# Four-head pass order, an early gate split before the Runge-Kutta loop, and 41 unread matmuls

## The reference

```python
x1 = ln(x) * (1 + scale1) + shift1                 # ada = cond @ ada_w + ada_b
x  = x + gate1 * (attention(x1, 16 heads of 128) @ out_w + out_b)
x2 = ln(x) * (1 + scale2) + shift2
x  = x + gate2 * (gelu(x2 @ ffn_w1 + b1) @ ffn_w2 + b2)     # block 1

z, h = sigmoid(x @ Wz.T + bz), g(x @ Wn.T + bn)    # block 2, minGRU:
s[t] = (1 - z[t]) * s[t-1] + z[t] * h[t]           # a scan over 32 tokens
drive = input + s

for t in range(32):                                # block 3: 32 RK4 steps
    for stage in range(4):                         # FitzHugh-Nagumo, state q, p
        dq = q - q**3/3 - p + drive[t] + tanh(q) @ coupling.T + bias
        dp = 0.08 * (q + 0.7 - 0.8 * p)
    q, p = clip(...)
    trace[t] = q
out = drive + blocksparse_ffn(trace)               # block 4, top 4 of 16 blocks
```

## Time and profile before

| what | value |
|---|---|
| median of 3 runs | 519.38 us (519.37 to 520.13) |
| the profiled execution: its time, its span | 521.38 us, 519.5 us |
| PE, DVE, ACT, POOL busy | 449.8, 434.4, 314.2, 48.4 us |
| chain that ended last, by engine | DVE 43%, PE 37%, ACT 10%, issue 5%, POOL 2%, DMA 2% |
| attention passes | to about 248 us |
| first and last write of q in the loop | 331.1 us, 507.4 us |

### The profile page before, as it was taken

How to read it: one execution, slowest core, us unless ns; L and a number is a source line. 1 busy time by engine, 2 the same in 40 slices (tenths; PEclk the granted TensorE clock), 3 DMA queues, 4 the chain that set the end, 5 groups by cost and what they waited for, 6 DMA issues and landing times.

```text
span 519.5 us, 13419 instructions
## 1 busy us (share of the span) xinstructions
PE 449.8 (87%) x4832; PEld 310.7 (60%) x4832; DVE 434.4 (84%) x1698; ACT 314.2 (60%) x872; POOL 48.4 (9%) x77
## 2 busy tenths in 40 slices
PE   2999989999999899997498996589797887888886
PEld 2655675557546665566244442478676776767676
DVE  4969876777776876979978776999999999999994
ACT  1378855786487748775467935464655646555563
POOL 2001320224021211042000000000000000000000
PEclk9899999999999999999789999596979879788899
DMA  8972402200202000000000000000000000000000
GB/s 292 415 305 62 105 4 78 61 21 0 81 21 61 0 1 0 0 1 0 0 1 1 0 1 0 3 2 0 2 1 11 11 0 11 1 11 11 1 10 22
DMA packets 10127, 20.82 MB, mean 40 GB/s; under 512 B 1456, under 2 KB 4720, under 8 KB 9456
## 3 DMA queue, kind: packets, MB, share of 16 engines
q1 hardware_dynamic: 9536, 19.89, 11.4%
q10 hardware_dynamic: 560, 0.60, 0.3%
HBM read 19.40 MB, written 1.08 MB: 39 GB/s over the span
## 4 chain that ended last, share of the span: by engine, by line
DVE 43%; PE 37%; ACT 10%; issue 5%; POOL 2%; DMA 2%; ACTq 0%; DVEq 0%
PE bank L765 33%; DVE base L1567 5%; DVE lin L1659 5%; DVE qs L1573 4%; DVE cub L1561 3%; DVE sq L1555 3%; ACT ptx L567 3%; PE score L765 3%; ACT ao_sb L535 2%; DVE pacc L1669 2%; POOL ptx L471 2%; ACT sraw L560 2%; PE spare L765 2%; DMA vec<-vecs 2%; DVE thlo L1551 1%
## 5 line engine op out<-in xcount | busy, mean ns | idle before, releaser
L765 PE MATMUL bank<-x,pairs_store 128*128 128x512 f16 x384 | 87.2, 384 | 0.0
L765 PE MATMUL score<-th,coup_part 128*128 128x32 f16 x1024 | 48.1, 182 | 19.4 <-ACT th L728 17.3
L765 PEld LDWEIGHTS bank<-x,pairs_store 128*128 128x128 f16 x384 | 37.7, 99 | 43.8 <-issue 2.2
L471 POOL TENSOR_TENSOR ptx<-pt,ptx 32x256 f16<-32x256 f32 x64 | 44.5, 696 | 190.8 <-ACT ptx L567 187.2
L535 ACT ACTIVATE big<-bank,pass_b 128x512 f16<-128x512 f32 x64 | 42.1, 683 | 23.5 <-DVE pass_b L1286 15.8
L728 ACT ACTIVATE th<-qs 128x64 f16<-128x64 f32 x96 | 24.4, 254 | 50.5 <-DVE qs L1573 50.5
L765 PEld LDWEIGHTS score<-th,coup_part 128*128 128x128 f16 x1024 | 36.4, 100 | 30.8 <-ACT th L728 29.3
L1298 DVE SCALAR_TENSOR_TENSOR big<-bank,pass_b,big 128x512 f16<-128x512 f32 x64 | 45.2, 739 | 7.5 <-ACT big L535 7.3
L765 PE MATMUL bank<-pairs_store,ao_sb 128*128 128x256 f16 x384 | 46.1, 273 | 5.2 <-DVE ao_sb L1298 1.9
L765 PEld LDWEIGHTS bank<-pairs_store,ao_sb 128*128 128x128 f16 x384 | 35.8, 98 | 12.7 <-DVE ao_sb L1298 4.3
L765 PE MATMUL bank<-pairs_store,x 128*128 128x512 f16 x192 | 43.4, 379 | 0.0
(11 more groups left out here) (197 smaller groups left out, 1017.9 us busy)
## 6 DMA issues: line engine op xcount, KB each, us to landing
wqk_sb<-wqk SPq DMA_DIRECT2D x16, 256.0 KB, 2.9
wv_sb<-wv SPq DMA_DIRECT2D x4, 512.0 KB, 5.7
wo_sb<-wo SPq DMA_DIRECT2D x4, 512.0 KB, 3.9
f_sb<-ffn_w SPq DMA_DIRECT2D x2, 1024.0 KB, 14.1
ao_sb<-xtok SPq DMA_DIRECT2D x4, 256.0 KB, 5.7
big<-ada_w SPq DMA_DIRECT2D x1, 1024.0 KB, 9.6
x_sb<-xT SPq DMA_DIRECT2D x1, 1024.0 KB, 13.4
w_sb<-w1T SPq DMA_DIRECT2D x1, 1024.0 KB, 16.2
```

The lines of the kernel that those rows point to most:

```text
L471: nc.gpsimd.tensor_tensor(ptx[s, 1, :, s], pt[s], ptx[s, 0, :, s], ALU.subtract).then_inc(ptx_ready, 1)
L765: return nc.tensor.matmul(dst, lhsT, rhs, start=start, stop=stop, **kw)
```

## The change

It has three parts.

1. **End of each attention pass.** ACT empties three of the four `project(3)` banks before `exps(2)`, and copies the two strips of scores 3 before `place_high(2)`. DVE does `low_projs(3)` and the first half of `low_pv(1)` before `normalise(2)`, the second half after `shift(3)`; `add_heads(0, 0)` comes after `normalise(3)`, and `add_heads(0, 3)` after `add_heads(1, 0)`.
2. **Gates of the second half and the entry of the loop.** `last_gates` splits piece n = 2 in two halves of 256 tokens, issues the products of feature block k = 0 before the last x3 is there, and puts the first half of Wn's product in `spare`. `min_gru` runs in halves for n = 2; for n = 3 ACT makes `za`. `drive_bias(1)`/`drive_lows(1)` go ahead of `residual(1)`. Of pieces 2 and 3 only the first four time steps are split before the loop; the other 28 go in eight parts into slots of the first iteration that before held a split of h with no use. The two tanh of the first stage stand before the loop, and each later pair at the end of the stage before, so that the loop's back-edge on ACT lies behind them.
3. **Unread matmuls.** 6, 15 and 20 matmuls of 512 fp16 columns whose results nothing reads: after `turn_x2(0)`, after `turn_normed(0)`, and after the last gate.

```diff
-                empty_projs(3, [0])
+                empty_projs(3, (0, 1, 2))
                 exps(2)
-                empty_projs(3, (1, 2, 3))
+                empty_projs(3, [3])
                 empty_pv(1)
+                copy_scores(3, NB4 // 2)
                 place_high(2)
-                copy_scores(3, NB4 // 2)
                 exps(3)
...
+            drive_bias(0, 1)
+            drive_bias(1, 2)
+
+            use = USE_GRU[1]
+            act.wait_ge(half_full, 1)
+            relu_pair(2, 2, first_half, 0, spare, half_ready)
+            wait_product(use + 1)
+            gate_tanh(2, first_half, 0, half_ready)
+            wait_product(use)
+            relu_pair(2, 3, second_half, 0, bank[bank_of(use)], free[bank_of(use)])
+            gate_tanh(2, second_half, 0, free[bank_of(use + 1)])
...
+            nc.scalar.activation(za_last, tz_of[1], ACT.Identity, bias=one_half[:], scale=-0.5).then_inc(za_ready, 1)
+            drive_bias(2, 4)
+            act.wait_ge(q_ready, 1)
+            nc.scalar.activation(th16[:], qn[:].rearrange("p k b -> p (k b)"), ACT.Tanh).then_inc(th16_ready, 1)
+            nc.scalar.activation(th32[:], qn[:].rearrange("p k b -> p (k b)"), ACT.Tanh).then_inc(th32_ready, 1)
+            drive_bias(3, 5, slice(0, UNROLL))
+            drive_bias(3, 5, slice(UNROLL, T))
...
+            def unread(dst, count):
+
+                for _ in range(count):
+                    mm(dst, scaled_eye[:], ptx[:, 0, 0:G // 2].rearrange("p g n -> p (g n)"), True, True)
+
+            pe.wait_ge(eye_ready, 1)
             turn_x2(0)
+            unread(spare[:], 6)
             turn_normed(0)
+            unread(spare[:], 15)
...
+            def last_gates():
+
+                dst = [fill(USE_GRU[1] + w) for w in range(2)]
+                middle = HALF // 2
+                wn_half = (spare[:, 0:middle], dst[0][:, middle:HALF])
+                pe.wait_ge(x3_ready, KB + 1)
+                for c in range(2):
+                    gate(0, c)
+                mm(dst[1][:], wz_sb[:, 0, 0:P], x3[:, 0, HALF:N], True, False)
+                pe.wait_ge(x3_ready, 2 * KB)
+                gate(1, 0).then_inc(half_full, 1)
+                mm(dst[1][:], wz_sb[:, 1, 0:P], x3[:, 1, HALF:N], False, True).then_inc(full[bank_of(USE_GRU[1] + 1)], 1)
+                gate(1, 1).then_inc(full[bank_of(USE_GRU[1])], 1)
...
             output_layer(1)
-            gates(1)
+            last_gates()
+            unread(score[:, 1], 20)
...
                 shift(2)
+                low_projs(3)
+                low_pv(1, [0])
                 normalise(2)
-                low_projs(3)
-                low_pv(1)
                 last_strips()
                 shift(3)
+                low_pv(1, [1])
+                normalise(3)
                 add_heads(0, 0)
-                normalise(3)
                 low_pv(2, [0])
...
+            min_gru(2, 2, first_half, (half_ready, 1), (half_ready, 2))
+            dve.wait_ge(z_used, 3)
+            min_gru(2, 3, second_half, emptied(use), emptied(use + 1))
+            dve.wait_ge(z_used, 4)
+            min_gru(3, 4, every, emptied(use + 2), emptied(use + 3), (za_ready, 1))
+            drive_lows(2, 3, slice(0, UNROLL))
+            drive_lows(3, 4, slice(0, UNROLL))
```

More of the change, by code:

```diff
@@ L133, in build @@
         eps_gelu = sb("eps_gelu", [P, 1])
+        one_half = sb("one_half", [P, 1])
         x1 = sb("x1", [P, KB, N])
@@ new lines, in gate_tanh, with wait_product @@
+            def gate_tanh(n, cols, ob, ready):
+                nc.scalar.activation(tz_of[n % 2][:, cols], bank[bank_of(USE_GRU[n // KB] + 2 * ob + 1)][:, cols], ACT.Tanh,
+                                     bias=hb[:, ob:ob + 1], scale=0.5).then_inc(ready, 1)
+            def wait_product(use):
+                act.wait_ge(full[bank_of(use)], count_of(use))
+            every, first_half, second_half = slice(0, HALF), slice(0, HALF // 2), slice(HALF // 2, HALF)
+            for ob in range(KB):
+                use = USE_GRU[0] + 2 * ob
+                wait_product(use)
+                relu_pair(ob, ob, every, ob, bank[bank_of(use)], free[bank_of(use)])
+                wait_product(use + 1)
+                gate_tanh(ob, every, ob, free[bank_of(use + 1)])
@@ L1591, in top_k, with later_drive @@
                 ins.then_inc(topk_step, 1)
+            def later_drive(piece, part):
+                first, width = UNROLL + piece % 4 * LATER, LATER
+                times = {None: slice(first, first + width), 0: slice(first, first + width // 2),
+                         1: slice(first + width // 2, first + width)}[part]
+                drive_lows(2 + piece // 4, 3 if piece < 4 else 5, times, None if part == 0 else h_low_ready)
             def split_h(n, m, part=None):
+                if n == 0:
+                    later_drive(m - 5 if m >= 5 else m + 3, part)
+                    return
                 count = MB * n + (m + 4 if m < 5 else m - 4)
@@ L1679, in _ @@
                 stage(t, 0, 1.0, q0, pscaled[:, 0], lambda: scaled(0),
-                      second=None if t else lambda: drive_lows(KB * NH - 1), late=True)
+                      late=True)
                 line(0, q0, 1.0 - H1 * ROWS[1][1], 1)
```

137 lines of the change are left out of this document (77 added, 60 removed).

## The result

The changed kernel takes 517.07 us (median of 6 runs, 516.00 to 517.89) against 519.82 for the kernel before on the same chip (6 runs, 519.37 to 523.08). The ratio is 0.9919, 95% interval 0.9893 to 0.9946: faster by 0.8%, or 2.75 us. The forecast was 514.8 us, with a range of its own of 514.0 to 515.7 and 517.0 as the upper end with the rivals. The profiled execution has a span of 515.7 us and took 517.44.

The account below looks back on a forecast made before the run. The prediction saw a chain alternating between DVE and PE, with a serial entry to the loop. Terms 0.4 + 0 + 4.2 + 0.1 - 0.1 = 4.6 us gave 514.8 us; range 514.0 to 515.7, with rivals 513.4 to 517.0.

Parts of the forecast that it names:

- rival of the pass order: End of a pass: POOL's room of 0.15 is too small, 2.0 us less gained, 516.8 us; chance 0.11.
- Entry, 4.2 forecast: Gates to loop: first q at 326.9 against 331.08, 4.2 us gained, bounds 2.8 to 4.6.
- for 256 I get 2.4: Entry: DVE needs 2.4 us for a half piece of 256, against 4.1 for a piece of 512.
- forecast's last step: Entry, first stage: base needs pscaled, issued behind ACT's 28-step conversion; pscaled at 326.45, base 326.5, q 326.9.
- Pass order, +0.4 forecast: End of a pass: place_high(3) at 180.40 instead of 180.54; 0.1 us gained a pass, 0.4 in all.
- Moving add_heads(1, 0) ahead [...] : 0: out_project: one bank is freed sooner, but PE waits for add_heads(1, 1) instead; 0 us.
- 0.15 of room: End of a pass: POOL keeps 0.15 of 0.9 us before mix(2)'s last 8 matmuls, so pv(2) still starts at about 179.2.
- Layer norm, 0 forecast: Second layer norm: unread matmuls raise PE's clock, but GELU 2 waits for DVE; value 0, bounds -1.3 to 0.
- What it would have made of the time, 2.9 us: MLP of the second layer norm: full clock shrinks 13.30 to about 10.4, 2.9 us more gained, 511.9; rival's chance 0.04.
- Clock at the entry, 0.1 forecast: First loop stages: 20 unread matmuls keep PE's clock up; 0.1 us gained, bounds 0 and 0.5.
- Loop, -0.1 forecast: ACT's back-edge now lies between tanh and pscaled; 0.1 us lost over seven back-edges, bounds 0 and -1.5.
- price of the slots, forecast at 0: Loop: eight later_drive slots of 112 elements take 0.29 for the 0.28 of the splits they replace; 0 us.

Follow-up runs that it names:

- e2: The kernel before with the change's pass order (ACT's and DVE's) alone; 522.29 us, ratio 1.0026 to the kernel before.
- e7: The kernel before with one edit: DVE empties the first bank of project(3) ahead of normalise(2); 519.68 us, ratio 0.9954 to the kernel before.
- e11: The kernel before with one edit: DVE empties all four banks of project(3) ahead of normalise(2); 520.81 us, ratio 0.9994 to the kernel before.
- e14: The changed kernel with e7's pass order and 30 and 40 unread matmuls in place of 15 and 20; 516.43 us, ratio 0.9915 to the kernel before.
- e3: The kernel before with the new entry of the loop alone; 517.51 us, ratio 0.9937 to the kernel before.

## Why the forecast was right in kind and where it was off

**Where the median lies.** 517.07 us is above the forecast's own range of 514.0 to 515.7 and nearest to the rival of the pass order (516.8, chance 0.11). Taken as a difference, 2.75 us below the kernel before on the same chip against 4.6 forecast, the way was right and the size too large by two thirds: the entry gave 0.6 less and the passes lost where a gain was added.

**Entry, 4.2 forecast, 3.63 measured.** Counted from x3, the forecast's points against the trace:

| point | forecast | measured |
|---|---|---|
| DVE starts the first half | 2.05 | 2.05 |
| DVE starts piece 3 | 7.05 | 7.38 |
| piece 3 done | 10.8 | 11.30 |
| `drive_low` full | 11.4 | 12.10 |
| PE starts | 11.8 | 12.46 |
| first `pscaled` ready | 12.35 | 12.83 |
| base starts | 12.4 | 13.08 |
| first q | 12.8 | 13.44 |

The mechanism was right and sizes were off. The term "for 256 I get 2.4" cost 2.64 and 2.61 (316.02 to 318.24 + 0.42, and 318.70 to 320.89 + 0.42): 0.33 too little with the gap between them, and piece 3 took 3.92 instead of 3.75. "Two of 0.2" for the splits of 64 elements was 0.31 and 0.33, the second 0.55 behind the first. The fixed part of a short DVE instruction is larger than was worked out. The forecast's last step held: base waits for `pscaled` behind the 28-step conversion, not for PE. It came 0.48 late, all of it from the pieces before. What the forecast left out there is a term: two slots of `later_drive` stand in the first stage, and the one ahead of base puts it 0.2 further back (base 0.68 late). With "from base to q 0.42", measured 0.36, that makes the 0.64.

**Pass order, +0.4 forecast, -0.37 measured (-0.45 in e2).** In passes 2 and 3 every start of the forecast up to head 3 came: mix(1) without its wait, pv(1) 1.1 earlier, place_high(2) later by 0.67 counted from the pass (0.75 forecast), pv(2) 0.03 later, place_high(3) 0.14 earlier. Two steps failed. "Moving add_heads(1, 0) ahead [...] : 0" was wrong: it costs 0.17 in `out_project` in each of the first three passes, so passes 2 and 3 end level (55.95 and 55.96 for 55.93 and 55.94) and only the last, which has no next pass, keeps 0.15. And the first pass was taken to be like the others. It takes 56.42 for 55.94. Its scores(2) wait for DVE in their second half and project(3) follows late, so there scores(3) came only 0.7 us earlier in the pass, place_high(2) 1.14 later, and place_high(3) 0.32 later instead of 0.14 earlier. The rival "the pass order loses" named POOL's room; POOL was indeed the last to end in the third pass (the 0.64 of PE's wait), but there pv(2) lost only 0.03. The 0.15 of room was not there: the last 8 matmuls stood 36.47 behind the start of the pass before, not 36.57, and 36.48 in the change, right behind POOL's end at 36.43. The rival had the sign, at a fifth of its price. e7 shows what the forecast's picture missed: 0.73 us a pass could be had by moving one bank, since pv(1) and with it place_high(2) come earlier and normalise(2) has room for that much; all four banks (e11) push normalise(2) past its room and take 0.6 of it back.

**Layer norm, 0 forecast, 0.02 measured.** Right, for the reason given. In one detail the count was off: the second MLP layer follows DVE's low part of the fourth GELU behind the second normalisation (273.63 to 274.32), not the fifth GELU. The rule of the Trainium skill, page "TensorE: Matmul & The Clock Gate", section on the oscillation of the gate, that an engine should be kept from idling, works as it says here: the granted clock was 1.00 instead of 0.50. What it would have made of the time, 2.9 us, did not come, and e14 shows that even a late start of PE costs nothing at that place.

**Clock at the entry, 0.1 forecast, 0 measured.** PE has 1.00 at its first stage in the change and 0.50 in e3; the first q comes after 13.44 and 13.43 us. DVE, held by `pscaled` and its slots, does not wait for PE there, and in the change too the clock is down to 0.50 again from about 328.3.

**Loop, -0.1 forecast, +0.17 measured.** The 0.17 is no finding: kernels with the same loop lie 0.44 apart (176.37 before, 176.81 in e7). ACT's back-edge is hidden: the seven stages at a back-edge sum to 10.07 us, to 10.08 before. The price of the slots, forecast at 0, was too low: 112 elements cost 0.40 instead of 0.29, and the seven stages of the first iteration with a slot were 0.04 to 0.15 longer than before, 0.66 in sum. The first iteration as a whole is only 0.34 longer, since in it the kernel before has an idle stretch of DVE of 0.24 and a back-edge 0.10 longer.

**Median.** 3.6 and -0.4 give 3.2 us; the medians of one chip differ by 2.75. The forecast of 514.8 took 4.6 us off the median of 519.38 of three runs. Of the 2.3 us between 514.8 and 517.07 the entry makes 0.57 and the passes 0.8; the kernel before was itself 0.44 slower on this chip (519.82 for 519.38), and the remaining 0.5 lies in start, loop and tail.

## What to carry to other kernels

When a bank or a buffer is waited for, move just the instruction that frees that one, into a gap in which the engine's next chain hasn't begun, and leave the chain's order alone: one moved instruction gave 2.9 us where a reordering of a dozen lost 0.4. Before lifting TensorE's clock, look who is waited for behind it; a faster engine ahead of the same last wait is only idle longer. A serial stretch shortens by starting on half a product and by putting off what the first step doesn't need, but price short instructions from the shortest ones in the trace, and keep what was put off out of the first stage too: here two slots stood in it.
